# Cross-attention and a low-rank mixture on one core: pair scores as 512 columns, the sum of their halves on VectorE, context loads in even steps, softmax scores ahead of the low parts

## The chip, the cores and the metric

The kernel runs on one core of a Trainium2 chip. The metric is the device time of one execution in microseconds (us). A profile of one execution stands beside the times. It names the engines PE (TensorE's matmuls; PEld is its weight load), DVE (VectorE), ACT (ScalarE), POOL (GpSimd) and SP (SyncE, whose queue issues most DMAs; SPq and ACTq are the rows in which DMAs are issued).

## What is computed

Eight batches of 1024 rows of 1024 elements. Each row is normalized, scored against its batch's 64 context rows, and the softmax-weighted context is added to it. The result is normalized again and goes through a dense layer, to which a mixture of rank-16 experts, the best two of eight, is added.

```python
def xattn(hidden_states, memory_tokens, memory_mask):
    scores = jnp.einsum('bsd,bmd->bsm', hidden_states, memory_tokens) * scale
    scores = jnp.where(memory_mask[:, None, :], scores, neg_inf)
    attn = jax.nn.softmax(scores, axis=-1)
    readout = jnp.einsum('bsm,bmd->bsd', attn, memory_tokens)
    ...
x = x + xattn(layernorm(x), ctx_2048, mask)
x = x + ffn(layernorm(x), weight, lora_A, lora_B, router_w)
# ffn: x @ weight.T, plus 2.0 * sum over the top 2 experts of gate * (x @ A.T) @ B.T
```

## The kernel before, in words

The 8192 rows are 64 tiles of 128, eight tiles to a batch; a tile is named (b, j). Each engine has its program written out by hand, a `step` per tile, and the engines meet only at semaphores. The order of the work is therefore the order of the calls in each `step`. Batches 1 to 6 run in a loop; batch 0 and the last one are written out.

A step of tile j on PE (`step`, L1243 on) first multiplies the normalized rows with two groups of weight columns (`base` for groups 0 and 1), then, where j is odd, takes the scores of the pair of tiles j+3 and j+4 (`pair_scores`), then tile j+2's readout, the third group, and the experts' second product (`lora_second`). Every factor is split in a high and a low part, and a product is hi·hi + hi·lo + lo·hi. `base` of the next tile may start only when the first half of that tile's low part is there: it waits for the semaphore `x2T_split`, which DVE raises in `x2T_low`.

`pair_scores` (L1139) holds the context as the stationary operand, its high and low part side by side in 128 columns (`ctxT`), and streams the transposed rows: for each of 8 chunks of the 1024 features a matmul with the pair's 256 high columns and one with its 256 low columns, all added up in the first 256 columns of the bank `s_ps`, which has 512.

What follows on DVE in the same odd step: `s_transposes` (L886) transposes `s_ps` in blocks of 32 into `sq`; SP (`s_exchange`, L420) waits for it and moves the blocks between partitions with four DMAs, which land in `s_raw`; then `softmax_scores` (L842) of tile j+3 waits for these four DMAs (`s_loaded`) and forms the scores in two scalar_tensor_tensor instructions and a maximum. For the pair's second tile this is done in the next, even step. From the maximum ACT takes the exponentials, DVE splits and transposes them, SP exchanges them, ACT copies them, and PE reads out.

DVE's step (L1001) ends with `x2T_low` (L932) of tile j+1, in two halves, then in some steps work on the next batch's context, then `softmax_scores` of tile j+3; behind it `add_bases` adds the finished products of tile j to its rows. The next batch's context is prepared in steps 3 to 6: sums of its transposed form in step 3 (`ctx_sum_chunks`), centring and split in step 4, its mask in step 5 and the low part of its plain form in step 6 (`ctx_low`, ahead of the router's work).

SP loads the next batch's context in step 1, behind the two loads of transposed rows of that step: the plain form with its mask (`load_ctx`, 520 KB) and then the transposed form (`load_ctxT`, 256 KB).

Of the kernel before, what the change touches and what calls it, by code (L numbers as in the profile page):

```python
# [23 lines left out]
def xattn_lora_moe_kernel(  # L24
# [66 lines left out]
    def after(tile, n):  # L91
        return (tile[0], tile[1] + n)
# [19 lines left out]
    with stack:  # L112
# [83 lines left out]
        sq = w_raw[0][:, C - 2, 0:T2]  # L196
        s_raw = w_raw[0][:, C - 3, 0:T2].rearrange("p (i k c) -> p i k c", i=Q, k=2)
# [126 lines left out]
        e_loaded = sem("e_loaded")  # L324
        sq_done = sem("sq_done")
# [27 lines left out]
        def _(sp):  # L353
# [73 lines left out]
            def step(tile, first=False):  # L427
# [24 lines left out]
                if j == 1 and exists((b, TPB)):  # L452
                    sp.wait_ge(ctx_split, b + 1)
                    sp.wait_ge(mask_step, b * 3 + 3)
                    load_ctx(b + 1)
                    sp.wait_ge(ctxT_split, b + 1)
                    load_ctxT(b + 1)
# [75 lines left out]
        def _(act):  # L533
# [94 lines left out]

            def hT_high(tile):
                act.wait_ge(h_loaded, count(tile, 16 * Q, 16 * Q * (1 - 2)))  # L630
                act.wait_ge(base_done, count(tile, G))
                act.copy(hT_hi[:, :], h[:, :]).then_inc(hT_hi_done, 1)
# [36 lines left out]
            def step(tile):  # L669
# [19 lines left out]
                if h_is_late(tile):  # L689
                    hT_high(tile)  # L690
                if exists(nxt):
                    x2T_high(nxt)
# [80 lines left out]
        def _(dve):  # L773
# [112 lines left out]
            def s_transposes(tile):  # L886
                dve.wait_ge(sT_done, pairs(tile, 1, 1))
                dve.transpose(sq.rearrange("p (j k c) -> p k j c", k=2, c=QP),
                              s_ps[:, 0:T2].rearrange("p (j c k) -> p k j c", k=2, c=QP)).then_inc(sq_done, 1)
# [111 lines left out]
            def step(tile):  # L1001
# [33 lines left out]
                if exists(nxt2):  # L1035
                    norm2_moments(nxt2)
                if exists(nxt):
                    x2T_low(nxt)
# [6 lines left out]
                elif exists(after(tile, 3)):  # L1045
                    softmax_scores(after(tile, 3))
# [68 lines left out]
        def _(pe):  # L1115
# [23 lines left out]
            def pair_scores(tile):  # L1139
# [5 lines left out]
                for c in range(C):  # L1145
                    pe.matmul(s_ps[:, 0:T2], ctxT[:, c, :], xT_hi[:, :, c, :].rearrange("p t n -> p n t"),  # L1146
                              start=(c == 0), stop=False)
                    mm = pe.matmul(s_ps[:, 0:T2], ctxT[:, c, :], xT_lo[:, :, c, :].rearrange("p t n -> p n t"),  # L1148
                                   start=False, stop=(c == C - 1))
# [257 lines left out]
```

## Time and profile before

| | us |
|---|---|
| median of 3 runs (981.21 to 981.75) | 981.63 |
| the profiled execution | 982.01 |
| its span, from the first to the last instruction | 980.1 |
| PE busy | 972.0 |
| DVE busy | 851.1 |
| ACT busy | 471.6 |
| POOL busy | 141.2 |

PE's granted clock is 1.00 of the full 2.4 GHz in every stretch of the steady loop. PE's busy time counts pipelined matmuls whose ends are modelled, so that what a matmul costs a stream is the distance from its start to the next one's start, and not its length. DVE's rows overlap by some hundredths of a microsecond in the same way.

### The profile page before, as it was taken

The page shows a single profiled execution, that of the slowest core. Times are in us where ns is not written, and L with a number is a line of the kernel's source. Part 1 is how long each engine was busy: PE and PEld are TensorE (multiplying, and loading weights), DVE is VectorE, ACT ScalarE, POOL GpSimd, SP SyncE. Part 2 cuts the span into 40 slices and gives each one's busy share as a digit, 9 for nine tenths or more (in the row PEclk, how much of TensorE's full clock was granted, in tenths as well). Part 3 has the DMA queues.
Part 4 walks back from the last instruction along what each step waited for, and adds up shares of the span by engine and source line. Part 5 has one row for each costly group of instructions (what it writes and reads, how often), then busy time and mean ns, then how long its engine had stood idle before and what let it go on. Part 6 is the DMA issues. An engine that isn't in the chain of part 4 may idle for free.

```text
span 980.1 us, 18830 instructions
## 1 busy us (share of the span) xinstructions
PE 972.0 (99%) x6081; PEld 960.0 (98%) x6081; DVE 851.1 (87%) x2201; ACT 471.6 (48%) x930; POOL 141.2 (14%) x278
## 2 busy tenths in 40 slices
PE   8999999999999999999999999999999999999998
PEld 7999999999999999999999999999999999999998
DVE  6989988899988998989988899888999889888774
ACT  7755544445444455435444445454454444444420
POOL 3311111111111111111111111111111111111110
PEclk9999999999999999999999999999999999999999
DMA  8646666656576566575656665666765576665532
GB/s 323 230 130 156 160 169 161 186 137 161 151 177 188 146 130 157 162 203 150 162 127 158 202 159 154 140 154 176 178 151 158 124 192 167 161 161 125 123 71 71
DMA packets 156096, 156.62 MB, mean 160 GB/s; under 512 B 93968, under 2 KB 128912, under 8 KB 156048
## 3 DMA queue, kind: packets, MB, share of 16 engines
q1 hardware_dynamic: 137616, 138.63, 52.0%
q10 hardware_dynamic: 18432, 17.45, 9.5%
q8 instruction: 18, 0.29, 0.1%
q14 instruction: 30, 0.25, 0.1%
HBM read 78.74 MB, written 33.55 MB: 115 GB/s over the span
## 4 chain that ended last, share of the span: by engine, by line
PE 94%; DVE 3%; DMA 1%; issue 1%; ACT 1%; POOL 0%; SPq 0%; DVEq 0%; ACTq 0%; POOLq 0%
PE base_ps L1119 27%; PE base_ps L1120 27%; PE base_ps L1121 27%; PE ro_ps L1193 3%; PE ro_ps L1194 3%; PE s_ps L1148 3%; PE s_ps L1146 3%; PE base_ps L1225 1%; DMA xq<-xn 1%; DVE stats L913 1%; DVE x2T L929 0%; DVE w_raw L907 0%; DMA ctxT_raw<-in_ctxT 0%; DVE ctx_sum L790 0%; PE s_ps L1156 0%
## 5 line engine op out<-in xcount | busy, mean ns | idle before, releaser
L1119 PE MATMUL base_ps<-w_hi,xT_hi 128*128 128x392 f32 x1512 | 495.6, 328 | 0.8 <-DVE xT_lo L936 0.8
L1120 PE MATMUL base_ps<-w_lo,xT_hi 128*128 128x392 f32 x1512 | 494.4, 327 | 0.0
L1121 PE MATMUL base_ps<-w_hi,xT_lo 128*128 128x392 f32 x1512 | 494.4, 327 | 0.0
L1119 PEld LDWEIGHTS base_ps<-w_hi,xT_hi 128*128 128x128 f32 x1512 | 285.8, 189 | 2.8 <-issue 1.0
L1120 PEld LDWEIGHTS base_ps<-w_lo,xT_hi 128*128 128x128 f32 x1512 | 285.8, 189 | 1.6
L1121 PEld LDWEIGHTS base_ps<-w_hi,xT_lo 128*128 128x128 f32 x1512 | 285.8, 189 | 0.0
L929 DVE STREAM_TRANSPOSE x2T<-xq 128x512 f32<-128x512 f32 x122 | 166.5, 1472 | 18.1 <-DMA xq<-xn 18.0
L495 POOL TENSOR_TENSOR rstd<-var_eps,neg_half 128x1 f32<-128x1 f32 x64 | 61.7, 964 | 391.4 <-DVE var_eps L920 391.4
L622 ACT CAST xT_hi<-x2T 128x512 fp32r<-128x512 f32 x122 | 69.5, 617 | 99.0 <-DVE x2T L929 99.0
L936 DVE TENSOR_TENSOR xT_lo<-x2T,xT_hi 128x512 fp32r<-128x512 f32 x122 | 78.3, 683 | 0.0
L610 ACT ACTIVATE xn<-w_raw,shift,rstd 128x1024 f32<-128x1024 f32 x32 | 39.7, 1241 | 77.3 <-POOL shift L498 77.3
L829 DVE TENSOR_TENSOR xT_parts<-xT_raw,xT_parts 128x1024 fp32r<-128x1024 f32 x62 | 73.4, 1185 | 0.0
L610 ACT ACTIVATE xn<-x_first,shift,rstd 128x1024 f32<-128x1024 f32 x29 | 36.0, 1241 | 76.5 <-POOL shift L498 76.5
L489 POOL TENSOR_TENSOR var_eps<-sum_sq,eps_sum 128x1 f32<-128x1 f32 x64 | 13.5, 211 | 391.8 <-ACT x2T L562 390.8
L571 ACT CAST xT_parts<-xT_raw 128x1024 fp32r<-128x1024 f32 x64 | 63.8, 1042 | 0.0
L591 ACT CAST eT<-w_raw 128x128 fp32r<-128x128 f32 x59 | 17.6, 298 | 95.7 <-DMA w_raw<-w_raw 95.7
L1119 PE MATMUL base_ps<-b_hi,hT_hi 128*128 128x384 f32 (+1 forms) x192 | 59.7, 311 | 0.0
L1120 PE MATMUL base_ps<-b_lo,hT_hi 128*128 128x384 f32 (+1 forms) x192 | 59.3, 309 | 0.0
L1121 PE MATMUL base_ps<-b_hi,hT_lo 128*128 128x384 f32 (+1 forms) x192 | 59.3, 309 | 0.0
L1148 PE MATMUL s_ps<-xT_parts,ctxT 128*128 128x256 f32 x232 | 53.3, 275 | 0.0
L1146 PE MATMUL s_ps<-xT_parts,ctxT 128*128 128x256 f32 x232 | 53.2, 275 | 0.0
L944 DVE MAX8 top<-base_ps 128x8 f32<-128x8 f32 x64 | 11.2, 175 | 46.0 <-PE base_ps L1121 45.5
(132 smaller groups left out, 1389.8 us busy)
## 6 DMA issues: line engine op xcount, KB each, us to landing
xT_raw<-in_xT SPq DMA_DIRECT2D x62, 512.0 KB, 5.3
w_raw<-in_x SPq DMA_DIRECT2D x32, 512.0 KB, 3.5
out<-x_first SPq DMA_DIRECT2D x32, 512.0 KB, 2.9
out<-w_raw SPq DMA_DIRECT2D x31, 512.0 KB, 2.8
xq<-xn SPq DMA_DIRECT2D x122, 128.0 KB, 4.1
xq<-xn ACTq DMA_DIRECT2D x122, 128.0 KB, 4.1
x_first<-in_x SPq DMA_DIRECT2D x30, 512.0 KB, 3.6
h<-w_raw SPq DMA_DIRECT2D x248, 16.0 KB, 1.8
```

Source lines behind the costliest of these rows:

```text
L495: pool.tensor_tensor(rstd2[:, :], var_eps2[:, :], neg_half[:, :], ALU.pow).then_inc(rstd2_done, 1)
L571: act.copy(xT_hi[:, i], xT_raw[:, k, i]).then_inc(xT_hi_done, 1)
L610: act.activation(xn[:, :], x(tile), ACT.Identity, bias=shift2[:, :], scale=rstd2[:, :]).then_inc(xn_done, 1)
L622: act.copy(chunks(xT2_hi[:, tile[1] % 2], i), chunks(x2T, i)).then_inc(x2T_hi_done, 1)
L829: dve.tensor_tensor(xT_lo[:, i], xT_raw[:, tile[1] // 2 % 2, i], xT_hi[:, i].bitcast(f32), ALU.subtract).then_inc(xT_split, 1)
L929: dve.transpose(out_[:, i * QS:(i + 1) * QS], xq[:, i * QS:(i + 1) * QS, :].rearrange("p g (c n) -> p g c n", n=QP)).then_inc(x2T_done, 1)
L936: dve.tensor_tensor(chunks(xT2_lo[:, k], i), chunks(x2T, i), chunks(xT2_hi[:, k], i).bitcast(f32), ALU.subtract).then_inc(x2T_split, 1)
L1119: pe.matmul(out_, a_hi, w_h, start=start, stop=False, skip_group_check=again)
L1120: pe.matmul(out_, a_hi, w_l, start=False, stop=False, skip_group_check=again)
L1121: return pe.matmul(out_, a_lo, w_h, start=False, stop=stop, skip_group_check=again)
L1146: pe.matmul(s_ps[:, 0:T2], ctxT[:, c, :], xT_hi[:, :, c, :].rearrange("p t n -> p n t"), start=(c == 0), stop=False)
L1148: mm = pe.matmul(s_ps[:, 0:T2], ctxT[:, c, :], xT_lo[:, :, c, :].rearrange("p t n -> p n t"), start=False, stop=(c == C - 1))
```

## The change

`pair_scores` becomes one matmul per chunk over 512 columns, 256 high ones and 256 low ones, whose products fall into the two halves of `s_ps`. So the halves have to be added: ACT copies the second half to `s_low` (`s_low_copy`, in its odd step behind the copy of `eT`), and DVE adds it to the first half in `s_sum`, which it then transposes. SP loads the transposed context in step 0 and the plain one in step 2, each behind that step's `s_exchange`. DVE forms the softmax scores ahead of `x2T_low`.

```diff
+        s_sum = w_raw[0][:, C - 4, 0:T2]
+        s_low = w_raw[0][:, C - 5, 0:T2]
...
         @block.sync  # step
-                if j == 1 and exists((b, TPB)):
+                if j == 0 and exists((b, TPB)):
+                    sp.wait_ge(ctxT_split, b + 1)
+                    load_ctxT(b + 1)
+                if j == 2 and exists((b, TPB)):
                     sp.wait_ge(ctx_split, b + 1)
                     sp.wait_ge(mask_step, b * 3 + 3)
                     load_ctx(b + 1)
-                    sp.wait_ge(ctxT_split, b + 1)
-                    load_ctxT(b + 1)
...
         @block.scalar
+            def s_low_copy(tile):
+                act.wait_ge(sT_done, pairs(tile, 1, 1))
+                act.copy(s_low, s_ps[:, T2:2 * T2]).then_inc(s_low_copied, 1)
...
+                if j % 2 == 1 and exists(after(tile, 3)) and not turned_on_pe(after(tile, 3), 6):
+                    s_low_copy(after(tile, 3))
                 if exists(nxt):
                     x2T_high(nxt)
...
         @block.vector
             def s_transposes(tile):
-                dve.wait_ge(sT_done, pairs(tile, 1, 1))
+                dve.wait_ge(s_low_copied, pairs(tile, 1, 1 - 3))
+                dve.tensor_tensor(s_sum, s_ps[:, 0:T2], s_low, ALU.add).then_inc(s_sum_done, 1)
+                dve.wait_ge(s_sum_done, pairs(tile, 1, 1 - 3))
                 dve.transpose(sq.rearrange("p (j k c) -> p k j c", k=2, c=QP),
-                              s_ps[:, 0:T2].rearrange("p (j c k) -> p k j c", k=2, c=QP)).then_inc(sq_done, 1)
+                              s_sum.rearrange("p (j c k) -> p k j c", k=2, c=QP)).then_inc(sq_done, 1)
...
                 if exists(nxt2):
                     norm2_moments(nxt2)
+                if not h_is_late(tile) and exists(after(tile, 3)):
+                    softmax_scores(after(tile, 3))
                 if exists(nxt):
                     x2T_low(nxt)
...
                 if turned_on_pe(after(tile, 3), 6):
                     first_softmax_scores(after(tile, 3))
-                elif exists(after(tile, 3)):
-                    softmax_scores(after(tile, 3))
...
         @block.tensor  # pair_scores
                 for c in range(C):
-                    pe.matmul(s_ps[:, 0:T2], ctxT[:, c, :], xT_hi[:, :, c, :].rearrange("p t n -> p n t"),
-                              start=(c == 0), stop=False)
-                    mm = pe.matmul(s_ps[:, 0:T2], ctxT[:, c, :], xT_lo[:, :, c, :].rearrange("p t n -> p n t"),
-                                   start=False, stop=(c == C - 1))
+                    mm = pe.matmul(s_ps[:, :], ctxT[:, c, :], xT_parts[:, :, :, c, :].rearrange("p k t n -> p k n t"),
+                                   start=(c == 0), stop=(c == C - 1))
```

DVE in an odd step of the loop, before. `sq`, `s_sum`, `s_low` and `s_raw` all lie in `w_raw`; L888 is the transposition, L913 to L921 the second normalization's statistics, L936 `x2T_low`, L850 to L858 the softmax scores, L999 `add_bases`.

```order
L888 STREAM_TRANSPOSE w_raw<-s_ps 128x2x4x32 [waits sT_done]
L907 SCALAR_TENSOR_TENSOR x_first<-ro_ps,e_scale,x_first 128x512 [waits readout_done,softmax_step]
L907 SCALAR_TENSOR_TENSOR x_first<-ro_ps,e_scale,x_first 128x512 [waits readout_done]
L913 BN_STATS stats<-x_first 128x6 [waits x1_done]
L921 TENSOR_SCALAR neg_mean<-mean_var 128x1
L936 TENSOR_TENSOR xT_lo<-x2T,xT_hi 128x512 [waits x2T_hi_done] x2
L850 SCALAR_TENSOR_TENSOR s_part<-w_raw,rstd,mask_bias 128x64 [waits s_loaded,rstd1_done]
L854 SCALAR_TENSOR_TENSOR s_all<-w_raw,rstd,s_part 128x64 [waits softmax_step]
L858 TENSOR_REDUCE neg_max<-s_all 128x1 [waits softmax_step]
L999 TENSOR_TENSOR w_raw<-base_ps_1,w_raw 128x256 [waits base_done]
```

The same step of the changed kernel, whose lines from there on are numbered 10 to 13 higher (L899 is the new addition, L901 the transposition, L949 `x2T_low`, L861 to L869 the scores):

```order
L899 TENSOR_TENSOR w_raw<-s_ps,w_raw 128x256 [waits s_low_copied]
L901 STREAM_TRANSPOSE w_raw<-w_raw 128x2x4x32 [waits s_sum_done]
L920 SCALAR_TENSOR_TENSOR x_first<-ro_ps,e_scale,x_first 128x512 [waits readout_done,softmax_step]
L920 SCALAR_TENSOR_TENSOR x_first<-ro_ps,e_scale,x_first 128x512 [waits readout_done]
L926 BN_STATS stats<-x_first 128x6 [waits x1_done]
L934 TENSOR_SCALAR neg_mean<-mean_var 128x1
L861 SCALAR_TENSOR_TENSOR s_part<-w_raw,rstd,mask_bias 128x64 [waits s_loaded,rstd1_done]
L865 SCALAR_TENSOR_TENSOR s_all<-w_raw,rstd,s_part 128x64 [waits softmax_step]
L869 TENSOR_REDUCE neg_max<-s_all 128x1 [waits softmax_step]
L949 TENSOR_TENSOR xT_lo<-x2T,xT_hi 128x512 [waits x2T_hi_done] x2
L1012 TENSOR_TENSOR w_raw<-base_ps_1,w_raw 128x256 [waits base_done]
```

The addition stands between PE's scores and the transposition, and the wait for `s_loaded` moved from behind the two instructions of `x2T_low` to ahead of them.

ACT in the same odd step of the changed kernel (L596 copies `eT`, L627 is the high part of the next tile's rows, L576 that of a later pair's):

```order
L596 CAST eT<-w_raw 128x128 [waits readout_done,e_loaded]
L636 COPY w_raw<-s_ps 128x256 [waits sT_done]
L627 CAST xT_hi<-x2T 128x512 [waits x2T_done]
L627 CAST xT_hi<-x2T 128x512
L641 CAST hT_hi<-h 128x128 [waits base_done,h_loaded]
L576 CAST xT_parts<-xT_raw 128x1024 [waits sT_done,xT_loaded1_0]
```

The second row is new; ahead of it and behind it ACT's order is that of before.

## Rows read from the trace of the kernel before

**Rows 1.** Windows, steps 1, 2, 4, 6: length; busy PE, PEld, DVE, ACT, POOL.

```profile
399.98:415.72 15.74, 15.74 (x103) 15.63 (x103) 13.62 (x37) 8.36 (x16) 2.02 (x4) 1.00 0.59 144
415.72:429.67 13.95, 13.95 (x87) 13.84 (x86) 12.22 (x32) 5.54 (x14) 2.02 (x4) 1.00 0.64 164
...
445.41:459.75 14.34, 14.34 (x88) 14.04 (x88) 13.85 (x36) 6.66 (x14) 1.83 (x4) 1.00 0.64 166
...
475.49:489.44 13.95, 13.95 (x87) 13.84 (x86) 13.35 (x33) 5.73 (x14) 2.02 (x4) 1.00 0.66 173
```

**Rows 2.** Waits, whole run: us in total, times, longest us.

```profile
DVE top L944 <- PE base_ps L1121: 45.5, 43, 3.5
DVE x2T L929 <- DMA xq<-xn: 18.0, 29, 1.9
```

**Rows 3.** Timeline, PE, odd step from 399.98: start us, us, then the instruction.

```profile
407.86 0.27 PE L1146 MATMUL s_ps<-xT_parts,ctxT 128*128 128x256 f32 x1
...
409.53 0.28 PE L1148 MATMUL s_ps<-xT_parts,ctxT 128*128 128x256 f32 x1
409.64 0.38 PE L1193 MATMUL ro_ps<-ctx_hi,eT 128*128 128x512 f32 x1
...
410.51 0.33 PE L1119 MATMUL base_ps<-w_hi,xT_hi 128*128 128x384 f32 x1
...
415.72 0.33 PE L1119 MATMUL base_ps<-w_hi,xT_hi 128*128 128x392 f32 x1
```

**Rows 4.** Timeline, DVE, the same step.

```profile
409.84 0.45 DVE L888 STREAM_TRANSPOSE w_raw<-s_ps 128x256 f32<-128x256 f32 x1 [0.41 <-PE s_ps L1148]
410.35 1.41 DVE L907 SCALAR_TENSOR_TENSOR x_first<-ro_ps,e_scale,x_first 128x512 f32<-128x512 f32 x2
...
413.60 1.28 DVE L936 TENSOR_TENSOR xT_lo<-x2T,xT_hi 128x512 fp32r<-128x512 f32 x2
414.80 0.28 DVE L850 SCALAR_TENSOR_TENSOR s_part<-w_raw,rstd,mask_bias 128x64 f32<-128x64 f32 x1
...
415.57 0.88 DVE L999 TENSOR_TENSOR x_first<-base_ps,x_first 128x256 f32<-128x256 f32 x2
```

**Rows 5.** SP's four DMAs of that step; the fourth alone (window 412.3:412.8).

```profile
410.32 2.50 SPq L424 DMA_DIRECT2D w_raw<-w_raw  x4
```

```profile
L424 SPq DMA_DIRECT2D w_raw<-w_raw x1: 603/603/603, 412.2 to 412.2; - x1
...
DMA to landing us min/median/max: 1.9/1.9/1.9
```

**Rows 6.** One line's DMAs (L424), whole run.

```profile
DMA to landing us min/median/max: 1.9/2.2/3.4
```

**Rows 7.** Prices: lines L576 and L888 (ns min/median/max), then groups (busy us, mean ns).

```profile
L576 ACT COPY sT<-s_ps x2: 351/362/372, 36.5 to 56.6; 128x256 f32<-128x256 f32 x2
```

```profile
L888 DVE STREAM_TRANSPOSE w_raw<-s_ps x29: 449/451/513, 82.5 to 916.5; 128x256 f32<-128x256 f32 x29
```

```profile
L999 DVE TENSOR_TENSOR w_raw<-base_ps,w_raw 128x256 f32<-128x256 f32 x32 | 13.3, 416 | 0.7 <-PE base_ps L1121 0.7
```

```profile
L929 DVE STREAM_TRANSPOSE x2T<-xq 128x512 f32<-128x512 f32 x122 | 166.5, 1472 | 18.1 <-DMA xq<-xn 18.0
```

**Rows 8.** Timeline, all engines, where PE waited for a low part; DVE line L936.

```profile
71.46 1.28 DVE L936 TENSOR_TENSOR xT_lo<-x2T,xT_hi 128x512 fp32r<-128x512 f32 x2
...
72.29 0.40 PE L1119 MATMUL base_ps<-w_hi,xT_hi 128*128 128x392 f32 x1 [0.76 <-DVE xT_lo L936]
```

```profile
L936 DVE TENSOR_TENSOR xT_lo<-x2T,xT_hi x122: 679/683/693, 71.5 to 962.3; 128x512 fp32r<-128x512 f32 x122
```

**Rows 9.** Timeline, DVE, even steps: j = 2, then j = 6.

```profile
428.04 1.28 DVE L936 TENSOR_TENSOR xT_lo<-x2T,xT_hi 128x512 fp32r<-128x512 f32 x2
...
479.78 0.17 DVE L944 MAX8 top<-base_ps 128x8 f32<-128x8 f32 x1
...
487.69 1.28 DVE L936 TENSOR_TENSOR xT_lo<-x2T,xT_hi 128x512 fp32r<-128x512 f32 x2
```

More of the change, by code:

```diff
@@ L324, in xattn_lora_moe_kernel @@
         e_loaded = sem("e_loaded")
+        s_low_copied = sem("s_low_copied")
+        s_sum_done = sem("s_sum_done")
         sq_done = sem("sq_done")
```

## The prediction

> **What bounds the kernel.** I read the windows first, cut at the start of each tile's first weight product. PE is busy for the whole of every step, 15.74 us in an odd one and 13.95 in an even one, at the full clock [rows 1]. The waits say the same from the other side: DVE waits for PE's router logits 43 times, 45.5 us in all [rows 2]. So DVE has some 0.7 us of slack a step on average, and the kernel's time is PE's column count, as long as each thing PE asks for is there in time. What a change costs is then decided by the margin of the things that come last. For the start of the next tile's product that is the first half of the low part (`x2T_low`).
>
> In the odd step that starts at 399.98, the timelines of PE, DVE and SP give that margin. The 16 score matmuls run from 407.86, the last ends at 409.53 + 0.28 = 409.81 [rows 3]. DVE, which had waited 0.41 us for it, transposes from 409.84 to 410.29. Its chain of readout and statistics then brings it to `x2T_low` at 413.60, 3.25 us after 410.35 [rows 4]. A half takes 0.68 us, and where PE did wait for one, its matmul began 0.15 us after the half's end (71.46 + 0.68 = 72.14, start 72.29) [rows 8]. So PE could have gone on at 413.60 + 0.68 + 0.15 = 414.43, and goes on at 415.72 [rows 3]: the margin is 1.29 us.
>
> The second thing to see is the exchange. SP issues its first DMA at 410.32, 0.03 after the transposition. The fourth starts at 412.2 and lands 1.9 us later, at 414.1 [rows 5], 3.83 us after the transposition's end if both roundings are taken in the middle. The softmax scores, in this same step and of this same pair, start at 414.80 without waiting [rows 4]: what covers the landing is `x2T_low`, which ran in between.
>
> **The change, part by part.**
>
> *Wide scores.* Sixteen matmuls take 407.86 to 409.64, 1.78 us; four of 512 columns, the readout's, take 409.64 to 410.51, 0.2175 us each [rows 3]. Eight make 1.74 us: 0.04 less per pair, and over 29 pairs (the count of the transposition [rows 7]) 1.2 us less. PE's last score then ends at 407.86 + 7 × 0.2175 + 0.38 = 409.76.
>
> The Trainium skill's page TensorE: Matmul & The Clock Gate (Back-to-back issue gap) gives a sustained 131 ns for a matmul of 512 columns. By it the eight would take an estimated 1.05 us. The readout's rows show 217 ns for the same width here, so the sum goes by them.
>
> *Copy and addition.* ACT's copy of 256 columns from this bank took 0.36 us, DVE's addition of 256 columns from PSUM and SBUF 0.42, the transposition 0.45 [rows 7]. Its source is SBUF now; above, I bound it by the other transposition from SBUF, 1.47 us for 512 columns, so 0.74 for 256. I take 0.45, the row of its own shape and pattern. The hand-overs from PE to ACT and from ACT to DVE lie between 0.03 (409.81 to 409.84) and 0.15 (above); I take 0.07. In one engine's chain 0.03 passes. So: 409.76 + 0.07 + 0.36 + 0.07 = 410.26 starts the addition, 410.68 ends it, and the transposition lasts from 410.71 to 411.16, against 410.29 before: 0.87 later. ACT has room for the copy: the casts that it pushes back are read by `x2T_low` alone, which comes more than 3 us after the scores (413.60 [rows 4]).
>
> *Softmax scores first.* DVE's chain of readout and statistics now ends at 413.60 + 0.87 = 414.47. There it meets the wait for the exchange, which lands at 411.16 + 3.83 = 414.99; with 0.03, the scores start at 415.02. They take 0.77 us (414.80 to 415.57 [rows 4]). `x2T_low` begins at 415.79 and its first half is with PE 0.83 later, at 416.62. PE stood ready at 415.72 less the 0.04. **The odd step ends 0.90 us later than before**, 0.52 of which are DVE's idle wait, 0.77 the scores and 0.87 the addition's path, less the margin of 1.29 (the rest is rounding). This chain runs from PE's scores to PE's next product, so the delay comes back in every odd step with pair scores: 29 × 0.90 = 26.1 us. The 1.2 us of the wide scores lie inside it and do not come on top.
>
> *Even steps.* There the pair's second tile finds its scores landed, and only the 0.77 us move ahead: 428.04 + 0.77 + 0.83 = 429.64, and PE needs it at 415.72 + 13.95 = 429.67 [rows 1, 9]. No cost, with nothing to spare. In step 6 DVE also has the context's low part ahead of its router work. In step 5 `x2T_low` begins 415.79 − 413.60 = 2.19 later, what follows it only 2.19 − 0.77 = 1.42 later because the scores no longer lie between, and so step 6's router maximum comes at 479.78 + 1.42 = 481.20, where PE's own delay of 0.90 would have excused 480.68. From there to `x2T_low` DVE runs without a wait, 487.69 − 479.78 = 7.91 us [rows 9]; 481.20 + 7.91 + 0.77 + 0.83 = 490.71, and PE is ready at 489.44 + 0.90 = 490.34: 0.37 us. In step 4, which centring and split of the context already make 14.34 long here (0.39 over 13.95), the same 0.77 stand before the low part; between 0 and 0.5, I take 0.2. Seven batches prepare a next one: 7 × 0.57 = 4.0 us.
>
> *Loads.* Moving 776 KB of context out of step 1 should shorten DVE's waits for the exchanged rows (18.0 us in 29 waits [rows 2]), the long ones of up to 1.9 us above all. These lie ahead of PE's scores, on which DVE now waits anyway; SP's two new places come behind the scores' exchange and their waits are for work of a batch earlier. I put it at 0, between 0 and −2 us.
>
> **Sum.** 26.1 + 4.0 = 30.1 us on the profiled execution's 982.0 is 1012.1; the median lies 0.4 lower: 1011.7, rounded to **1011.5 us**.
>
> **Bounds.** Up: the transposition at 0.74 adds 0.29, hand-overs of 0.15 add 0.16, together 0.45 × 29 = 13 us: 1025. A landing of 3.4 us instead of 1.9 [rows 6] in a few steps goes the same way. Down: the case without any wait for the exchange, next.
>
> **Rivals.**
>
> *The exchange is not waited for.* If the four DMAs, issued at a quieter moment, land before DVE's 414.47, an odd step costs 414.47 + 0.77 + 0.83 − 415.72 = 0.35, 10.2 us in 29, with the even steps 14.2: 995. For it speaks that x's load, which SP issues shortly before, is further along when the exchange starts. Against it: 1.9 us is the least of the 4 × 29 landings [rows 6], and SP's issues take 1.9 us before it whatever else runs. Chance 0.09.
>
> The page DMA: Bandwidth & Descriptors (Rules for kernel authors) says to issue a DMA early, compute, and wait late, so that its fixed cost is covered; the change moves the wait ahead of the compute. The same page (Anatomy of one DMA) puts the fixed cost at about 2.0 us. By that figure alone, with the four issues side by side, an estimated landing at 413.2 would be covered after all and this rival's time would follow; the row's 3.83 us counts the issues one after another, and the sum goes by the row.
>
> *Faster: the low part is not what PE waits for.* The first half must be done by 415.68 − 0.15, so the scores must start by 414.08, which is 0.39 before DVE's own chain allows and 0.91 before the landing. It decides this way if the addition's path costs under 0.5 us instead of 0.87 and the exchange lands within 3.3 us of the transposition. Then 1.2 us of the scores and some 0.25 us of PE's gap in seven steps 4 are won: 979. For it: where DVE comes late for the scores, ACT's 0.36 us hide. Against: DVE waited for the scores here [rows 4], and the 3.83 us have no part that a quieter queue takes away. Chance 0.05.
>
> *Wide scores at 131 ns.* PE's last score would end 0.60 earlier and so would the whole chain, the odd step would cost 0.30, and the time would be 995. The readout's rows speak against it; chance 0.01.
>
> **Chances.** The forecast's mechanism (a wait on the exchange ahead of the low part) has 0.83, of its own range 1004 to 1023; the exchange unwaited 0.09; wide at 131 ns 0.01; faster 0.05; no change, where gains and stalls cancel within 0.2% (2 us, about what a measurement of this kernel tells from no change), 0.02. Slower sums to 0.93. The range from 997 to 1023 leaves out the last two, half of the second, and the tail above.
>
> **What would show it.** In the profile after: score matmuls of 512 columns 0.215 to 0.22 us apart, 29 × 8 of them; in odd steps an idle time of DVE of about 0.5 us before the first softmax score, put down to the DMA into `w_raw`; PE's first weight product of even tiles waiting for `xT_lo`, 0.8 to 0.95 us each, some 27 times; odd steps of 16.6 us and even ones still of 13.95, except j = 4 and 6. I am wrong if PE shows no wait for `xT_lo`, if odd steps stay under 16.0, or if the added DVE work itself makes even steps longer throughout.

## The result and the profile after

| | before | after |
|---|---|---|
| median | 981.64 (6 runs, 981.03 to 982.77) | 1013.97 (6 runs, 1013.66 to 1014.81) |
| the profiled execution, its span | 982.01, 980.1 | 1014.81, 1013.0 |

The change makes the kernel slower: the ratio is 1.033, its 95% interval 1.0319 to 1.0341. The prediction was 1011.5 us with a range from 997 to 1023.

The page of the kernel after, its first and its fourth part (busy time; the chain that ended last, by engine):

```profile
PE 979.8 (97%) x5849; PEld 950.9 (94%) x5849; DVE 870.0 (86%) x2230; ACT 479.2 (47%) x959; POOL 122.2 (12%) x278
...
PE 73%; DVE 10%; DMA 7%; SPq 5%; issue 2%; ACT 2%; POOL 0%; ACTq 0%; DVEq 0%; POOLq 0%
```

DVE, DMA and SP's queue now stand in the chain with 22% between them. In the kernel before, PE alone had 94% of that chain. PE is busy for 7.8 us more than before although it has 232 matmuls less. The busy time counts matmuls to their modelled ends, and the first one behind a wait counts 0.43 us instead of 0.33 (rows of the odd step below). So the 7.8 us do not stand for more work.

The windows of five steps of one batch of the kernel after, cut at the start of each tile's first weight product as in [rows 1], with the same columns: j = 0, 1, 2, 4, 6.

```profile
769.95:784.01 14.06, 14.06 (x86) 13.96 (x87) 12.71 (x34) 4.95 (x13) 1.99 (x4) 1.00 0.66 169
784.01:800.61 16.60, 15.84 (x95) 15.23 (x94) 13.70 (x36) 9.30 (x18) 1.47 (x4) 1.00 0.62 149
800.61:814.67 14.06, 14.06 (x86) 13.95 (x87) 12.71 (x34) 4.90 (x13) 1.99 (x4) 1.00 0.66 167
831.27:845.78 14.51, 14.51 (x87) 14.02 (x88) 13.85 (x36) 5.25 (x13) 1.99 (x4) 1.00 0.66 177
862.51:876.57 14.06, 14.06 (x86) 13.92 (x86) 13.57 (x35) 4.88 (x13) 1.99 (x4) 1.00 0.64 168
```

The odd step went from 15.74 to 16.60, and PE is idle for 0.76 us of it (16.60 less 15.84). The even ones went from 13.95 to 14.06. The clock is 1.00 as before, so it has no part in this.

The waits of the kernel after (us in total, times, longest):

```profile
DVE top L957 <- PE base_ps L1134: 41.5, 46, 3.5
PEld base_ps L1132 <- DVE xT_lo L949: 27.7, 30, 1.4
PE base_ps L1132 <- DVE xT_lo L949: 24.1, 31, 1.1
DVE s_part L861 <- DMA w_raw<-w_raw: 20.8, 29, 1.1
...
DVE x2T L942 <- DMA xq<-xn: 7.8, 23, 1.4
```

Two of these waits are new: DVE's for the exchanged scores, 29 times and 20.8 us, and PE's for the low part, 31 times and 24.1 us (in the kernel before once, [rows 8]). DVE's wait for the router's logits is still there 46 times. So DVE has slack in the mean step and is late in one place of every second step. An engine's busy share could not have told that.

The odd step from 413.58 of the kernel after, by engine: PE's scores and its readout, ACT's copy, then DVE, then SP, then PE's next tile.

```profile
421.46 1.89 PE L1159 MATMUL s_ps<-xT_parts,ctxT 128*128 128x512 f32 x8
423.18 0.38 PE L1204 MATMUL ro_ps<-ctx_hi,eT 128*128 128x512 f32 x1
...
423.38 0.37 ACT L636 COPY w_raw<-s_ps 128x256 f32<-128x256 f32 x1 [1.84 <-PE s_ps L1159]
...
423.79 0.42 DVE L899 TENSOR_TENSOR w_raw<-s_ps,w_raw 128x256 f32<-128x256 f32 x1 [0.53 <-ACT w_raw L636]
424.25 0.50 DVE L901 STREAM_TRANSPOSE w_raw<-w_raw 128x256 f32<-128x256 f32 x1
...
427.82 0.14 DVE L934 TENSOR_SCALAR neg_mean<-mean_var 128x1 f32<-128x1 f32 x1
428.69 0.28 DVE L861 SCALAR_TENSOR_TENSOR s_part<-w_raw,rstd,mask_bias 128x64 f32<-128x64 f32 x1 [0.73 <-DMA w_raw<-w_raw]
...
429.46 0.68 DVE L949 TENSOR_TENSOR xT_lo<-x2T,xT_hi 128x512 fp32r<-128x512 f32 x1
...
424.77 2.51 SPq L428 DMA_DIRECT2D w_raw<-w_raw  x4
...
430.20 0.43 PE L1132 MATMUL base_ps<-w_hi,xT_hi 128*128 128x392 f32 x1 [0.78 <-DVE xT_lo L949]
430.47 0.33 PE L1133 MATMUL base_ps<-w_lo,xT_hi 128*128 128x392 f32 x1
430.63 0.33 PE L1134 MATMUL base_ps<-w_hi,xT_lo 128*128 128x392 f32 x1
```

This is the predicted chain with each link in its place. PE's last score is followed by the copy, the addition and the transposition. Then SP issues four DMAs one after another, and DVE stands idle until the last has landed. Only then come the scores, the first half of the low part and PE. The wait in brackets ends DVE's idle time, and SP's row shows why it is so long: the fourth DMA is issued some 1.9 us after the first.

### The profile page after: what moved, and what is told of

Same layout as the page of the kernel before. It is cut to its first block, busy times and chain, and to the rows that moved or that the text cites. A ratio compares the mean times of both kernels' runs of the same rounds, so it can differ in the third digit from the quotient of the medians.

```text
span 1013.0 us, 18448 instructions
## 1 busy us (share of the span) xinstructions
PE 979.8 (97%) x5849; PEld 950.9 (94%) x5849; DVE 870.0 (86%) x2230; ACT 479.2 (47%) x959; POOL 122.2 (12%) x278
## 4 chain that ended last, share of the span: by engine, by line
PE 73%; DVE 10%; DMA 7%; SPq 5%; issue 2%; ACT 2%; POOL 0%; ACTq 0%; DVEq 0%; POOLq 0%
PE base_ps L1132 22%; PE base_ps L1133 21%; PE base_ps L1134 21%; DMA w_raw<-w_raw 6%; SPq L428 5%; PE s_ps L1159 5%; DVE xT_lo L949 2%; DVE w_raw L901 1%; PE ro_ps L1204 1%; PE ro_ps L1205 1%; DVE w_raw L899 1%; PE base_ps L1236 1%; ACT w_raw L636 1%; DVE s_all L865 1%; DVE s_part L861 1%
## 5 line engine op out<-in xcount | busy, mean ns | idle before, releaser
L1132 PE MATMUL base_ps<-w_hi,xT_hi 128*128 128x392 f32 x1512 | 500.1, 331 | 24.3 <-DVE xT_lo L949 24.1
L942 DVE STREAM_TRANSPOSE x2T<-xq 128x512 f32<-128x512 f32 x122 | 172.7, 1528 | 8.0 <-DMA xq<-xn 7.8
L627 ACT CAST xT_hi<-x2T 128x512 fp32r<-128x512 f32 x122 | 69.6, 620 | 77.5 <-DVE x2T L942 77.5
L500 POOL TENSOR_TENSOR rstd<-var_eps,neg_half 128x1 f32<-128x1 f32 x64 | 36.9, 577 | 409.8 <-DVE var_eps L933 409.8
L949 DVE TENSOR_TENSOR xT_lo<-x2T,xT_hi 128x512 fp32r<-128x512 f32 x122 | 78.3, 683 | 0.0
L631 ACT ACTIVATE gate_num<-top 128x1 f32<-128x1 f32 x64 | 18.9, 295 | 97.1 <-DVE top L957 96.9
L576 ACT CAST xT_parts<-xT_raw 128x1024 fp32r<-128x1024 f32 x64 | 63.9, 1046 | 0.0
L1159 PE MATMUL s_ps<-xT_parts,ctxT 128*128 128x512 f32 x232 | 54.8, 379 | 0.0
L1204 PE MATMUL ro_ps<-ctx_hi,eT 128*128 128x512 f32 x128 | 49.3, 385 | 0.3 <-ACT eT L596 0.3
L1205 PE MATMUL ro_ps<-ctx_lo,eT 128*128 128x512 f32 x128 | 48.6, 380 | 0.0
```

What stands on the lines that cost most here:

```text
L576: act.copy(xT_hi[:, i], xT_raw[:, k, i]).then_inc(xT_hi_done, 1)
L627: act.copy(chunks(xT2_hi[:, tile[1] % 2], i), chunks(x2T, i)).then_inc(x2T_hi_done, 1)
L942: dve.transpose(out_[:, i * QS:(i + 1) * QS], xq[:, i * QS:(i + 1) * QS, :].rearrange("p g (c n) -> p g c n", n=QP)).then_inc(x2T_done, 1)
L949: dve.tensor_tensor(chunks(xT2_lo[:, k], i), chunks(x2T, i), chunks(xT2_hi[:, k], i).bitcast(f32), ALU.subtract).then_inc(x2T_split, 1)
L1132: pe.matmul(out_, a_hi, w_h, start=start, stop=False, skip_group_check=again)
L1159: mm = pe.matmul(s_ps[:, :], ctxT[:, c, :], xT_parts[:, :, :, c, :].rearrange("p k t n -> p k n t"), start=(c == 0), stop=(c == C - 1))
```

## The experiments

The runs in one table. "Odd", "even" and "j = 4" are mean lengths of steps in batches 1 to 6, worked out from the starts of each tile's first weight product in the trace: 24 odd steps, 18 with j = 0, 2 or 6, and six with j = 4. The ratios are to runs of the kernel before on the same chip.

| kernel | us | ratio, 95% interval | odd | even | j = 4 |
|---|---|---|---|---|---|
| before | 981.64 | | 15.74 | 13.98 | 14.26 |
| after | 1013.97 | 1.0319 to 1.0341 | 16.66 | 14.08 | 14.48 |
| e1: after, scores behind the low part | 995.61 | 1.0126 to 1.0159 | 15.68 | 14.55 | 14.56 |
| e2: before, order changed alone | 991.99 | 1.0097 to 1.0131 | 15.89 | 14.07 | 14.47 |
| e3: after, exchange by SP and ACT | 1000.09 | 1.0164 to 1.0204 | 15.98 | 14.32 | 14.76 |
| e4: after, scores between the halves | 994.58 | 1.0113 to 1.0146 | 15.68 | 14.44 | 14.65 |
| e5: before, loads moved alone | 981.66 | 0.9992 to 1.0010 | 15.74 | 13.99 | 14.18 |
| e6: e5, context's work spread | 982.29 | 0.9998 to 1.0016 | 15.74 | 13.98 | 14.18 |
| e8: before, wide scores and addition alone | 996.94 | 1.0141 to 1.0172 | 15.68 | 14.53 | 14.59 |
| e9: wide, several steps moved | 1043.31 | 1.0616 to 1.0645 | 15.75 | 15.80 | 16.98 |
| e10: e1, half of e's exchange by POOL | 1014.01 | 1.0310 to 1.0344 | 15.68 | 15.22 | 15.23 |
| e11: after, half of both exchanges by POOL | 1013.44 | 1.0303 to 1.0338 | 15.87 | 15.12 | 15.09 |
| e12: before, half of e's exchange by POOL | 993.09 | 1.0099 to 1.0133 | 15.75 | 14.42 | 14.38 |
| e13: e1, half of e's exchange left out | 985.03 | 1.0020 to 1.0044 | 15.68 | 14.06 | 14.45 |

The table can be read by columns. Where the odd step is long, PE mostly waited for the low part. Where the even step is well over 14.1, it mostly waited for its readout.

**Three theories.** A: two margins are overdrawn, that of the low part ahead of PE's next product, and a second one ahead of PE's readout (the chain from the second normalization over the exchange of rows and of exponentials to `eT`). B: the order alone is to blame. C: the wide scores, or DVE's added work by itself, are to blame.

### The order undone (e1), and only half undone (e4)

e1 is the changed kernel with `softmax_scores` back behind `x2T_low`:

```diff
-                if not h_is_late(tile) and exists(after(tile, 3)):
-                    softmax_scores(after(tile, 3))
                 if exists(nxt):
                     x2T_low(nxt)
...
+                elif exists(after(tile, 3)):
+                    softmax_scores(after(tile, 3))
```

> The changed kernel with one part undone: softmax scores stand behind the low part again; wide scores, copy, addition and the moved loads stay. Theory A (two margins: the addition's path makes everything behind PE's scores 0.87 us later, which uses up most of the 1.29 us before PE's next product and all of the 0.3 to 0.4 us before PE's next readout; the order then added 0.77 and the exchange's wait): no wait of PE for the low part, but PE's readout of the even steps waits for eT by 0.5 to 0.7 us in 29 pairs, since the second normalization and the exchanges behind it are 0.87 later; about 998 us (994 to 1002). Theory B (the order alone is to blame, the addition hides): 979 to 981 us. Theory C (the wide scores or DVE's added work are to blame, the order is not): 1010 to 1015 us.

Measured: 995.61 us, as theory A had it. The odd step is 15.68, which is 0.06 less than before, the gain of the wide scores. The even step is 14.55. In e1's waits PE waits for something else:

```profile
PEld ro_ps L1204 <- ACT eT L596: 16.7, 29, 1.1
PE ro_ps L1204 <- ACT eT L596: 8.9, 26, 0.8
```

In e4 the scores stand between the two halves of `x2T_low`:

```diff
+                if exists(nxt):
+                    x2T_low(nxt, (0,))
                 if not h_is_late(tile) and exists(after(tile, 3)):
                     softmax_scores(after(tile, 3))
                 if exists(nxt):
-                    x2T_low(nxt)
+                    x2T_low(nxt, (1,))
```

> The changed kernel with softmax scores between the two halves of the low part: the first half is done before DVE asks for the exchange. Theory A (only the first half is what PE waits for at the start of its next product): no wait of PE for the low part; what is left is the readout's wait as in the first run of this call, so the same time as that one within 2 us, about 998 us (994 to 1002). If the second half matters as well: 1005 to 1014 us. Theory B: 978 to 981 us.

Measured: 994.58 us, e1's time within the intervals. So the first half of the low part is what PE waits for in the kernel after. With the rest of the change in place, the order accounts for about 18 us of its loss (1013.97 less 995.61), and the other 14 lie elsewhere.

### The parts alone (e2, e8, e5)

e2 is the kernel before with e1's lines the other way round.

> The kernel before with one part done alone: softmax scores ahead of the low part; narrow scores, no addition, loads where they were. Theory A: the exchange lands at its old place, DVE waits for it by about 0.5 us less than 0.1 us short of what PE can bear, so that PE waits 0.05 to 0.2 us per pair, and in steps 4 and 6 of seven batches 0.3 to 0.4 us each: 984 to 991 us. Theory B (the order alone is to blame): 1008 to 1014 us. Theory C: 980 to 983 us.

Measured: 991.99 us (990.43 to 994.75), just above theory A's range. Its waits:

```profile
DVE s_part L850 <- DMA w_raw<-w_raw: 18.3, 29, 1.2
...
PEld base_ps L1119 <- DVE xT_lo L936: 6.8, 25, 0.7
```

The narrow kernel's margin of 1.29 us is used up by the wait (18.3 / 29 = 0.63 us) and the scores (0.77). An odd step is 0.15 longer and an even one 0.09.

e8 is the kernel before with the wide matmul, `s_low_copy` and the addition; the order and the loads stay.

> The kernel before with wide scores, copy and addition alone; loads and order as before. Theory A (the loads hardly matter): within 2 us of the run with scores behind (995.6), 994 to 999 us. Rival (the moved loads cost in that run): 985 to 992 us.

Measured: 996.94 us, with e1's step lengths, as theory A had it. e5 is the kernel before with the loads moved.

> The kernel before with the context's loads moved to steps 0 and 2, nothing else. Theory A: DVE's long waits for exchanged rows in step 3 (1.2 to 1.9 us) shrink, but they end ahead of PE's scores, so PE gains only what steps 4 lose after them (14.34 and 14.53 us fall to 14.18): 980.5 to 981.8 us, a gain of 0 to 1 us. Rival (the loads' traffic delays exchanges all along): 976 to 979 us.

Measured: 981.66 us, no difference. Step 4 fell to 14.18 in every batch as expected, from 14.26 on average, but that makes only some 0.5 us over six batches.

The order alone costs 10 us, the wide scores with their addition 15 and the loads nothing. That is 25, while all of them together cost 32. The parts don't add up because they share a margin: either alone stays within the low part's 1.29 us or nearly so, and both together overdraw it by 0.9. The 0.55 us that the wide scores alone cost in an even step is then hidden: in the kernel after that step is 14.08.

### The exchange by two queues (e3)

SP issues two of the scores' four DMAs, and ACT the other two, at the end of its odd steps.

```diff
         @block.sync   # s_exchange
-                for i in range(Q):
+                for i in range(Q // 2):
...
         @block.scalar # step, at its end
+                if j % 2 == 1 and exists(after(tile, 3)) and not turned_on_pe(after(tile, 3), 6):
+                    s_exchange(after(tile, 3))
...
```

> The changed kernel, where two of the four DMAs of the scores' exchange are issued by ACT behind its copy of h, and two by SP; nothing else differs. Theory A (SP's issues one after another make the exchange 3.8 us long, and DVE's wait for it is 0.5 to 0.7 us of the 0.87 that PE loses in an odd step): the exchange lands before DVE asks, the odd step falls from 16.6 to about 16.1 us, part of it comes back in the even step's readout: about 1002 us (998 to 1006). Theory C (DVE's added work is to blame, the exchange is hidden): unchanged, 1012 to 1016 us.

Measured: 1000.09 us (997.92 to 1002.18), within theory A's range. The waits:

```profile
PEld base_ps L1140 <- DVE xT_lo L957: 12.0, 33, 2.2
PEld ro_ps L1212 <- ACT eT L596: 6.2, 18, 1.4
...
DVE s_part L869 <- DMA w_raw<-w_raw: 2.3, 2, 1.9
```

DVE's wait falls from 20.8 us to 2.3, and 14 us come back. From the transposition's end to the last landing the exchange now takes 2.9 us instead of 3.8 (medians of 29), so SP's issues in a row were part of its length, as the prediction had counted them. PE's waits for `eT` show up as those for the low part shrink: PE's delay in odd steps had hidden the second margin.

### The second margin (e13, e12, e10, e11)

These timelines show the second margin. First the kernel before, an even step; it starts at 415.72.

```profile
415.17 1.25 ACT L610 ACTIVATE xn<-x_first,shift,rstd 128x1024 f32<-128x1024 f32 x1 [2.46 <-POOL shift L498]
...
416.44 1.49 SPq L382 DMA_DIRECT2D xq<-xn  x2
...
417.97 2.57 SPq L418 DMA_DIRECT2D w_raw<-w_raw  x4
...
422.99 0.30 ACT L591 CAST eT<-w_raw 128x128 fp32r<-128x128 f32 x1 [1.35 <-DMA w_raw<-w_raw]
...
423.44 0.19 PEld L1193 LDWEIGHTS ro_ps<-ctx_hi,eT 128*128 128x128 f32 x1
423.60 0.38 PE L1193 MATMUL ro_ps<-ctx_hi,eT 128*128 128x512 f32 x1
```

Over the whole run of that kernel:

```profile
PEld ro_ps L1193 <- ACT eT L591: 1.3, 5, 0.4
```

Then the same rows of the timeline of e1, with the readout's second matmul, in an even step that starts at 421.50.

```profile
421.70 1.24 ACT L615 ACTIVATE xn<-x_first,shift,rstd 128x1024 f32<-128x1024 f32 x1 [2.58 <-POOL shift L503]
...
422.97 1.50 SPq L386 DMA_DIRECT2D xq<-xn  x2
...
424.52 2.57 SPq L422 DMA_DIRECT2D w_raw<-w_raw  x4
...
429.52 0.30 ACT L596 CAST eT<-w_raw 128x128 fp32r<-128x128 f32 x1 [2.09 <-DMA w_raw<-w_raw]
...
429.87 0.19 PEld L1204 LDWEIGHTS ro_ps<-ctx_hi,eT 128*128 128x128 f32 x1 [0.62 <-ACT eT L596]
429.87 0.48 PE L1204 MATMUL ro_ps<-ctx_hi,eT 128*128 128x512 f32 x1 [0.33 <-ACT eT L596]
...
430.19 0.38 PE L1205 MATMUL ro_ps<-ctx_lo,eT 128*128 128x512 f32 x1
```

In the kernel before `eT` is done at 423.29 and PE's weight load starts at 423.44: there is at most 0.15 us to spare, some 0.05 of which the hand-over itself takes (429.82 to 429.87 in e1). It is less than the 0.3 to 0.4 us that e1's and e6's texts give, and five times in the run it is not enough. SP issues the two row DMAs and then the four of the exponentials, all in a row, and in both kernels `eT` starts 7.82 us after `xn`. From the start of the odd step, `xn` starts at 415.17 − 399.98 = 15.19 before and at 421.70 − 405.82 = 15.88 in e1, which is 0.69 later: the addition's path has pushed back the whole second normalization. As e1's odd step is also 0.06 shorter, `eT` comes 0.75 later in the even step. PE's readout starts 0.49 later there (429.87 − 421.50 = 8.37 after the step's start, 423.60 − 415.72 = 7.88 before), and its second matmul follows after 0.32 instead of 0.22 us [rows 3]. That makes 0.59, and this even step is 14.55 long in e1 and 13.95 before.

That was still an argument. e13 takes the cause away: it is e1 with two of the four DMAs of `e_exchange` left out, and ACT's wait set to match.

```diff
         # e_exchange
-                for i in range(Q):
+                for i in range(Q // 2):
...
         # eT_copy
-                act.wait_ge(e_loaded, count(tile, 16 * Q, 16 * Q * (1 - 5)))
+                act.wait_ge(e_loaded, count(tile, 8 * Q, 8 * Q * (1 - 5)))
```

> The changed kernel with the scores behind the low part again, and with the last two of the four DMAs that exchange a tile's exponentials left out, so that half of eT holds old numbers; the columns that PE multiplies are the same. SP issues 1.25 us less and what ACT waits for is there that much earlier. If the readout's margin is what is left of the loss (995.6 us with all four DMAs), the waits for eT go and the time falls to 979 to 986. If the wide scores or DVE's addition cost the loss by themselves, it stays at 992 to 997.

Measured: 985.03 us, in the range for the readout's margin. PE's wait for `eT` and the even step:

```profile
PEld ro_ps L1204 <- ACT eT L596: 3.9, 11, 0.6
```

The even step falls from 14.55 to 14.06. Of the 13.9 us that e1 loses, 10.6 went with the two DMAs. Theory C can hold no more than the 3.3 us that remain, unless what else SP issues, which comes earlier here too, has hidden some of it; that is not shown.

The same margin from the other side: e12 is the kernel before, in which nothing changes but who issues two of those four DMAs: POOL does, at the end of its step and behind a small product of its own.

```diff
         # SP, e_exchange
-                for i in range(Q):
+                for i in range(Q // 2):
...
+            def e_exchange(tile):
+                pool.wait_ge(eq_done, count(tile, 1, 1 - 5))
+                pool.tensor_tensor(pool_gate[:, :], eps_sum[:, :], neg_half[:, :], ALU.mult)
+                for i in range(Q // 2, Q):
+                    pool.dma_start(e_raw[:, i * QP:(i + 1) * QP], eq[i * QP:(i + 1) * QP, :]).then_inc(e_loaded2, 16)
...
```

> The kernel before with only the exponentials' last two DMAs issued by POOL: the price of POOL's issuing by itself. In the kernel before PE waits neither for eT nor for a low part, so the theory of two margins says 981 to 982.5 if POOL's DMAs land no later than SP's; if they land more than 0.4 us later, PE's readouts wait and it gets slower than 984.

Measured: 993.09 us, 11 us more: POOL's DMAs land later, the second of the two cases. POOL's rows and PE's wait in e12:

```profile
406.94 1.08 POOL L504 TENSOR_TENSOR pool_gate<-eps_sum,neg_half 128x1 f32<-128x1 f32 x1 [2.67 <-DVE w_raw L895]
407.96 1.13 POOL L506 DMA_DIRECT2D w_raw<-w_raw  x2
```

```profile
PEld ro_ps L1204 <- ACT eT L602: 12.7, 30, 0.8
```

POOL's product ahead of its DMAs takes 1.08 us, and in even steps (j = 0, 2 and 6 of the loop) `eT` is done 8.18 us after the step's start instead of 7.58. These 0.60 us, off every engine that looks busy, cost 11 us, which shows how thin the margin was in the kernel before.

e10 (e1 with POOL's half) and e11 (the changed kernel with POOL's half in both exchanges) were meant to bring time back.

> The changed kernel with the scores behind the low part again, and the last two of the four DMAs that exchange a tile's exponentials issued by POOL instead of SP. If what is left of the loss there (995.6 us) is the readout's margin, that is, PE waiting for eT because SP issues this exchange in series behind the row exchange, then eT comes up to 1.2 us earlier (two issues of 0.6), PE's waits for it (25.6 us in 55 waits on PE and its weight loads) go, and the time falls to 980 to 987. If the wide scores or DVE's addition cost by themselves, it stays at 993 to 997. If POOL's DMAs land later than SP's third and fourth, it gets slower than 996; POOL has issued no DMA in any trace here, so that stands open beforehand.

> The changed kernel with its order kept, and the last two of four DMAs of both exchanges, the scores' and the exponentials', issued by POOL. If the two margins are all, the scores land some 1.2 us earlier, DVE no longer waits the 0.7 us for them, an odd step ends 0.2 to 0.4 late instead of 0.87, and readouts are in time: 986 to 996. If the exchange lands no earlier this way: 1008 to 1016. If DVE's added work itself costs what the changed kernel loses: over 1000 even with the wait gone.

Measured: 1014.01 and 1013.44 us. e10 came out by the case that its text had left open: what POOL issues comes later. Its even step grew to 15.22. e11 is the more useful one, and a miss: its time lies in the range for an exchange that lands no earlier, but only by luck. The scores' exchange does land earlier there, 2.9 us after the transposition instead of 3.8 (medians of 29), and the odd step is 15.87 instead of 16.66. Its even step is 15.12. So the one stall was cured and the other made worse, and the time stood still. Its waits:

```profile
PEld ro_ps L1226 <- ACT eT L617: 26.1, 29, 2.4
...
PEld base_ps L1154 <- DVE xT_lo L971: 7.7, 24, 0.6
```

### Attempts at a faster version (e6, e9)

e6 adds to e5: the context's sums from step 3 to step 4 (behind e's transposition), and ACT's `ctxT_high` behind `eT_copy`.

```diff
         # DVE
+                if j == TPB - 4 and exists((b, TPB)):
+                    ctx_sum_chunks(b + 1)
...
-                if j == TPB - 5 and exists((b, TPB)):
-                    ctx_sum_chunks(b + 1)
...
```

> The run before this one, and further the context's sums on DVE in step 4 behind the transposition of e instead of at the end of step 3, and ACT's high part of the transposed context behind its copy of eT. Narrow scores, order as before. Theory A (PE's readout has a margin of 0.3 to 0.4 us, which these two take up in step 4, 0.23 us and more in seven batches): step 4 falls to 13.95 us, 978.5 to 980.3 us. Rival (step 4's gap comes from the exchange itself): no change against the run before.

Measured: 982.29 us, a miss. Its step 4 is 14.18, as in e5, so the 0.2 us that this step has over other even ones don't come from where these sums stand. PE's rows in a step 4 of the kernel before show what they are:

```profile
330.39 0.33 PE L1126 MATMUL h_ps<-ctx_sum,one_dth 128*128 128x64 f32 x2
330.53 0.41 PE L1119 MATMUL base_ps<-w_hi,xT_hi 128*128 128x384 f32 x1
330.78 0.33 PE L1120 MATMUL base_ps<-w_lo,xT_hi 128*128 128x384 f32 x1
```

In this step alone PE multiplies out the mean of the next batch's context. The two matmuls take 0.14 us to the next start, and the one behind them 0.25 instead of 0.16 or 0.17: 0.22 us of PE's own time, the same in e5 and e6. Neither theory had this.

e9 is a wide kernel in which the addition and transposition stand behind `norm2_moments`, the scores' exchange is shared by SP and ACT, odd steps' scores stand behind `add_bases`, e6's spreading is in, and ACT issues its half of the row exchange ahead of the exponentials:

```diff
         # ACT, step
+                if exists(nxt):
+                    exchange(nxt)
                 if turned_on_pe(nxt2, 5):
                     first_softmax_exp(nxt2)
                 elif exists(nxt2):
                     softmax_exp(nxt2)
-                if exists(nxt):
-                    exchange(nxt)
...
```

> Wide scores with the addition's path taken off both margins: DVE adds and transposes behind the second normalization's moments, the exchange is issued by SP and ACT together, the softmax scores of odd steps stand behind the addition of the bases, ACT issues its rows' exchange ahead of the exponentials, context's work spread as in the run with the sums in step 4. Theory A (wide scores cost nothing once no margin is overdrawn, and save 0.04 us a pair): 977.5 to 982 us if the late scores still meet the readout, up to 990 if they miss it by some tenths. Rival (DVE's 0.9 us more work per pair costs time wherever it stands): 995 us and more.

Measured: 1043.31 us, a clear miss. ACT's rows at the start of one step, and then waits of DVE and PE over the run:

```profile
427.53 1.23 ACTq L621 DMA_DIRECT2D xq<-xn  x2
428.94 0.35 ACT L589 ACTIVATE e_all<-s_all,neg_max 128x64 f32<-128x64 f32 x1 [1.44 <-issue]
```

```profile
DVE e_split L897 <- ACT e_split L591: 89.8, 59, 2.6
...
PEld h_ps L1149 <- DVE ctx_sum L809: 15.4, 7, 3.5
```

Two DMAs issued by ACT hold up what stands behind them on ACT for 1.44 us. Here the exponentials stood behind them, and DVE, and behind DVE `eT`, for which PE waits. PE also waits for the context's sums, which were moved too. e9 moved too many things at once to price each of them. No version here beat the kernel before.

## Why the prediction was right, point by point

*Wide scores.* The predicted 1.74 us for eight matmuls is 1.72 in the rows: 421.46 to the readout's start at 423.18. That is 0.215 apart, at a granted clock of 1.00. For 512 columns the Trainium skill's page TensorE: Matmul & The Clock Gate (Back-to-back issue gap) gives a sustained distance of 131 ns, and by its formula for a matmul by itself an estimated 216 ns. The measurement decides against the first of these figures, on which the rival stood, and agrees with the second. The gain is real: odd steps of 15.68 in e1, e4 and e8.

*Copy and addition.* The transposition was to end at 411.16 in a step that starts at 399.98, 11.18 us after the start. Here it ends 424.75 − 413.58 = 11.17 after it. Two errors of a few hundredths cancel: the hand-overs took 0.03 and 0.04 instead of 0.07 each, and the transposition 0.50 instead of 0.45. The copy's 0.37 and the addition's 0.42 are as taken from [rows 7].

*The wait ahead of the scores.* Predicted 0.52, measured 20.8 / 29 = 0.72. DVE arrived 0.1 earlier than I had it, at 427.96 − 413.58 = 14.38 instead of 14.49, which costs nothing, and the scores started 0.07 later, at 15.11 instead of 15.04, 0.06 of which is the hand-over from the landing to DVE: 0.09 us instead of the 0.03 taken. Only the second counts.

*The odd step.* Predicted +0.90 and so 16.64, measured 16.62 in this step, 16.66 on average.

*Even steps.* Here two terms were mis-sized. I had put these steps at nothing except for j = 4 and j = 6. All of them are 0.1 longer: after a stall PE's first matmul stands 0.27 us before the next (430.20 to 430.47), where the following ones stand 0.16 apart. No other distance between PE's starts has grown in such a step, so it is not DVE's work that makes it longer. The 0.37 of step 6 did not come; in five of six batches that step is 14.06 like the others, in one 14.39. DVE's rows in the one that starts at 862.51:

```profile
867.10 0.17 DVE L957 MAX8 top<-base_ps 128x8 f32<-128x8 f32 x1
...
875.74 1.28 DVE L949 TENSOR_TENSOR xT_lo<-x2T,xT_hi 128x512 fp32r<-128x512 f32 x2
```

The router's maximum comes 867.10 − 862.51 = 4.59 us after the step's start, 0.30 later than before, where the prediction's 481.20 stands for 0.52 later. Two short waits that DVE has there in the kernel before, 0.16 us ahead of the split of the exponentials and 0.14 ahead of this maximum (by the distances between starts), took up the rest of its lateness. The first half is with PE at 875.74 + 0.83 = 876.57, just when PE goes on. So the step has no margin left, but costs nothing.

Step 4 grew by 0.22 where I took 0.2. The reading behind it was wrong, though. The prediction put the 0.39 by which that step is longer in the kernel before down to DVE's work on the context; 0.22 of it are PE's own two matmuls (the rows under e6), and the rest is a wait for `eT` in that batch. So the 0.25 us a batch that the rival "faster" counted on could not be won there.

*Sum.* A batch of the loop takes 4.20 us more (25.2 us in six), against 4 × 0.90 + 0.57 = 4.17 in the prediction, with 3.68 of it in odd steps, 0.30 in j = 0, 2 and 6, and 0.22 in j = 4. That it agrees to 0.03 is luck in part: the 0.30, which stood at nothing, came in place of the 0.37 of step 6. The median rose by 32.3 instead of 30.1. The rest lies outside the loop, where the profiled execution loses 7.7 us against 5 × 0.90 + 0.57 = 5.1 in the prediction. It is 5.0 us behind when batch 1 starts, 1.3 of which stand there from the first tile on (it starts at 22.51 against 21.22 us; in e1 and e4, which begin with the same instructions, at 21.00 and 22.24), so they are scatter and not the change's. The other 1.3 stay open.

*Loads.* Put at nothing, and e5 shows nothing. DVE's waits for the exchanged rows did shrink, from 18.0 us to 12.2 in e5 and 7.8 in the kernel after.

*What I had not seen.* The forecast would have been wrong for a kernel with a slightly different order. The prediction had one margin, the low part's, and put nothing on the readout's. In the kernel after, PE's own lateness in odd steps gives the readout back its time, so the second margin is hidden: `eT` is done 6.70 us after an even step's start there, 7.58 before and 8.31 in e1 (means over j = 0, 2 and 6 of the loop). But the rival "faster: the low part is not what PE waits for" priced a kernel with the low part in time at 979, and e1 and e4, in which it is in time, took 995. The delay of 0.87 us that I had followed to the low part also runs on through the second normalization into `eT`. The rival's chance of 0.05 was therefore too high, not too low.

*The exchange.* It took 428.59 − 424.75 = 3.84 us from the transposition's end to the last landing, predicted 3.83; a DMA lands 1.8, 1.9 and 2.5 us after its issue as minimum, median and maximum. The rival in which it is not waited for did not occur, and e3 shows what it would have given: the wait nearly gone, and 1000 us. (By their own terms the two rivals priced at 995 come to 996 and 994.) The Trainium skill's page DMA: Bandwidth & Descriptors (Rules for kernel authors) says to issue early, compute, and wait late. The trace agrees: e1 and the kernel after differ in whether the wait, with the 0.77 us of the scores, stands behind or ahead of the low part, and by 18 us. The 2.0 us that the prediction took from that page of the Trainium skill (Anatomy of one DMA) stands there for DMAs that GpSimd issues; SP's landed after a median of 1.9.

## What to carry to other kernels

Before moving a step on a busy engine, list every hand-over that PE waits for and how long each is ready beforehand: here the low part had 1.29 us and `eT` at most 0.15, and each move that looked free spent one of the two. A wait for a DMA belongs behind the work that covers it, and a row of DMAs on one queue takes as long as its issues, here 0.6 us each on SP. A part that is harmless alone can be dear together with another if both draw on one margin, and a delay in one place can hide a second shortage, so time won at the first may show up as a wait at the second.

## What the runs showed of the hardware that I had not expected

- After a stall, PE's first two matmuls start 0.27 us apart instead of 0.16 (0.32 instead of 0.22 for the readout's 512 columns, in e1), so a short wait costs some 0.1 us more than its length.
- The transposition of 128x256 takes 501 ns on average from SBUF here, against 466 from PSUM before, with the same pattern.
- An instruction of ACT behind two DMAs that ACT issued itself started 1.44 us late (e9).
- A one-column product on POOL, the one ahead of its DMAs in e12, took 1.08 us.
- With two of four DMAs of 16 KB issued by POOL, behind that product, instead of by SP, what waits for them came 0.60 us later (e12).
